# The L3 attention heads of a four-layer kernel: tiles handled in pairs, one reciprocal for two tiles

## The chip, the cores and the metric

The kernel runs on one core of a Trainium2 chip. The metric is the device time of one execution in microseconds (us): the median of 3 runs before the change is 2008.98 us (2007.1 to 2012.11).

## The reference, cut to what matters

Four conditioned layers, L0 to L3, follow each other on an activation of 2 x 1024 x 256. The change touches the attention of L3 alone:

```
qkv = (h @ Wqkv.T).reshape(b, n, 3, 16, 64)
q, k = _ln(q, qn_g, qn_b), _ln(k, kn_g, kn_b)        # per head, 64 wide
scores = einsum('bhnd,bhmd->bhnm', q, k) / sqrt(64)  # 1024 x 1024 per head
attn = softmax(scores, axis=-1)
o = einsum('bhnm,bhmd->bhnd', attn, v)               # then @ Wout.T, and a mixture of experts
```

There are 2 x 16 = 32 heads, each with a full 1024 x 1024 softmax over its rows.

## The kernel before

The stage `l3h` (class `Heads`, run by `heads_stage`) has one program for each engine. They run side by side and are tied only by semaphores. Its unit is a tile g: 128 query rows of one head against all 1024 keys. A head has TB = 8 tiles, and there are 256 tiles in all. For each tile:

- TensorE **scores** it (L1510): three passes of a high and low split of q and k, times two halves of the keys that stand on different rows of the array, into one of two score tiles in PSUM.
- VectorE takes the negated row maximum (L1567), ScalarE the exponential with the row sum (L1591), VectorE the reciprocal of the sum (L1573), and GpSimd scales the rows by it (L1601). The rows live in four slots of `prob`.
- TensorE **turns** it (L1521): 16 transposes of 64 rows x 128 columns, eight for each half of the rows. The halves go to two PSUM banks, `ring[0]` and `ring[1]`. VectorE copies one bank to `pT` (L1557), ScalarE the other (L1559).
- TensorE **mixes** (L1533): it multiplies a block of the turned rows with V, eight blocks kk for each head, into a result bank, which ScalarE copies out (L1581) and SyncE stores (L1479).

The order on each engine is written out by hand. Before, TensorE's loop over g does score(g), turn(g - 3), and the mix of the block 8 tiles behind the turn. VectorE does maximum g, reciprocal g - 1, copy g - 3. ScalarE does copy g - 3, exponential g. score(g) waits for the exponential of tile g - 2, whose score tile it overwrites. turn(g) waits until tile g is scaled and both banks of tile g - 1 are emptied.

SyncE's queue does, for each n: load q and k of head n + 1 (eight transfers, L1426 and L1427), store head n - 2, load V of head n + 1 (L1473). q and k have two buffers, and so has V. The load of V for head n + 1 first waits until `outs` counts n heads, that is until head n - 1 is mixed to its end. Only behind it in the same queue stand q and k of head n + 2. From n = 20 on, eight loads of finished heads for the next stage (L2069, `o3T`) stand in this queue too, one for each n. GpSimd has four pieces of weight splitting between its scalings, one each at tiles 40, 48, 56 and 64.

Of the kernel before, what the change touches and what calls it, by code (L numbers as in the profile page):

```python
# [18 lines left out]
ALU = mybir.AluOpType  # L19
ACT = mybir.ActivationFunctionType  # L20
AX = mybir.AxisListType

P = 128
B, S, D = 2, 1024, 256
T = B * S // P
TB = S // P
# [1085 lines left out]
def layer1_attention(nc, sems, g, w, nt):  # L1112
# [5 lines left out]
    with Stage(nc, sems, "l1att") as s:  # L1118
# [70 lines left out]
        @block.vector  # L1189
        def _(dve):  # L1190
            def empty(t):
                for half in range(2):
                    dve.wait_ge(his, 2 * t + half + 1)
                    dve.tensor_tensor(place(1, t, half), ring[half][:, :].rearrange("p (k q) -> p k q", k=TC),
                                      place(0, t, half).bitcast(F32), ALU.subtract).then_inc(emptied, 1)

            def residual(t):
                if t == 0:
                    dve.wait_ge(xbs, T)
                dve.reciprocal(inv[:, t:t + 1], total[:, t:t + 1]).then_inc(inverse, 1)  # L1200
                dve.wait_ge(outs, t + 1)
                dve.wait_ge(inverse, t + 1)
                dve.scalar_tensor_tensor(X[:, t, :], ob[t % 2][:, 0:D], inv[:, t:t + 1], X[:, t, :],
                                         ALU.mult, ALU.add).then_inc(added, 1)

            for t in range(T + 3):
                if t < T:
                    dve.wait_ge(scores, t + 1)
                    dve.tensor_reduce(nmax[:, t:t + 1], score[t % 2][:, :], AX.X, ALU.max, negate=True).then_inc(maxes, 1)
                if 1 <= t <= T:  # L1210
                    empty(t - 1)
                if t >= 3:
                    residual(t - 3)
                if T - 4 < t < T:
                    dve.wait_ge(added, (t - T + 4) * TC)
                    nt.dve_stats(dve, t - T + 3)
                if t == T:
                    nt.dve_norm(dve, 0)
# [210 lines left out]

class Heads:  # L1430

    LAG = 3
    N = B * H
    LOADS = 8

# [64 lines left out]
    def pe_program(self, pe):  # L1500
        def score(g):
            n, t = divmod(g, TB)
            u = n % 2
            if t == 0:
                self.need(pe, self.loaded[u], (n // 2 + u) * 16 * self.LOADS)
            self.need(pe, self.exps, g - 1)
            for i, (x, y) in enumerate(PASSES):
                for c in range(2):
                    r = slice(c * self.hd, (c + 1) * self.hd)
                    mm = pe.matmul(self.score[t % 2][:, c * C:(c + 1) * C], self.Q[u][r, x, t * P:(t + 1) * P],  # L1510
                                   self.K[u][r, y, :], start=i == 0, stop=i == 2)
            mm.then_inc(self.scores, 1)

        def turn(g):
            pe.wait_ge(self.scaled, g + 1)
            self.need(pe, self.emptied_d, g)
            self.need(pe, self.emptied_a, g)
            for kk in range(TB):
                for half in range(2):
                    r = slice(half * P // 2, (half + 1) * P // 2)  # L1520
                    mm = pe.transpose(self.ring[half][:, kk * P // 2:(kk + 1) * P // 2],  # L1521
                                      self.prob[r, g % 4, kk * P:(kk + 1) * P], self.ident[r, r])
                    if kk == TB - 1:
                        mm.then_inc(self.turned, 1)

        def mix(n, kk):
            if kk == 0:
                pe.wait_ge(self.emptied_d, TB * (n + 1))
                pe.wait_ge(self.emptied_a, TB * (n + 1))
                pe.wait_ge(self.vloaded[n % 2], 16 * (n // 2 + 1))  # L1530
                self.need(pe, self.ocopied, n - 1)
            for c in range(2):
                mm = pe.matmul(self.ob[n % 2][c * self.hd:(c + 1) * self.hd, :], self.vs[:, n % 2, kk, :],  # L1533
                               self.pT[:, n % 2, kk, c * C:(c + 1) * C], start=kk == 0, stop=kk == TB - 1)
            if kk == TB - 1:
                mm.then_inc(self.outs, 1)

        for g in range(TB * self.N + self.LAG + TB):
            if g < TB * self.N:
                score(g)  # L1540
            gt = g - self.LAG
            if 0 <= gt < TB * self.N:
                turn(gt)
            n, kk = divmod(gt - TB, TB)
            if n >= 0:
                mix(n, kk)

    def empty(self, eng, g, half):
        n, t = divmod(g, TB)
        eng.wait_ge(self.turned, 2 * g + half + 1)  # L1550
        if t == 0:
            self.need(eng, self.outs, n - 1)
        at = t * P + half * P // 2
        dst = self.pT[:, n % 2, :, at:at + P // 2]
        src = self.ring[half][:, :].rearrange("p (k q) -> p k q", k=TB)
        if half == 0:
            eng.tensor_copy(dst, src).then_inc(self.emptied_d, 1)  # L1557
        else:
            eng.activation(dst, src, ACT.Copy).then_inc(self.emptied_a, 1)  # L1559

    def dve_program(self, dve):
        for g in range(TB * self.N + self.LAG):
            if g < TB * self.N:
                t = g % TB
                dve.wait_ge(self.scores, g + 1)
                self.need(dve, self.exps, g - 3)
                dve.tensor_reduce(self.nmax[:, t % 4:t % 4 + 1], self.score[t % 2][:, :], AX.X, ALU.max,  # L1567
                                  negate=True).then_inc(self.maxes, 1)
            if 1 <= g <= TB * self.N:
                q = (g - 1) % 4  # L1570
                dve.wait_ge(self.exps, g)
                self.need(dve, self.scaled, g - 4)
                dve.reciprocal(self.inv[:, q:q + 1], self.total[:, q:q + 1]).then_inc(self.invs, 1)  # L1573
            if g >= self.LAG:
                self.empty(dve, g - self.LAG, 0)

    def act_program(self, act):
        def ocopy(n):
            act.wait_ge(self.outs, n + 1)
            self.need(act, self.stored[n % 2], 32 * (n // 2))  # L1580
            act.activation(self.osb[:, n % 2, :], self.ob[n % 2][:, :], ACT.Copy).then_inc(self.ocopied, 1)  # L1581

        for g in range(TB * self.N + self.LAG + 2 * TB):
            if self.LAG <= g < TB * self.N + self.LAG:
                self.empty(act, g - self.LAG, 1)
            if g < TB * self.N:
                q = g % 4
                act.wait_ge(self.maxes, g + 1)
                self.need(act, self.turned, 2 * (g - 3))
                self.need(act, self.invs, g - 3)  # L1590
                act.activation(self.prob[:, q, :], self.score[g % 2][:, :], ACT.Exp, bias=self.nmax[:, q:q + 1],  # L1591
                               accum_out=self.total[:, q:q + 1]).then_inc(self.exps, 1)
            n, k = divmod(g - 2 * TB, TB)
            if k == self.LAG - 1 and 0 <= n < self.N:
                ocopy(n)

    def pool_program(self, pool):
        for g in range(TB * self.N):
            q = g % 4
            pool.wait_ge(self.invs, g + 1)  # L1600
            pool.tensor_scalar(self.prob[:, q, :], self.prob[:, q, :], self.inv[:, q:q + 1], self.vscale,  # L1601
                               ALU.mult, ALU.mult).then_inc(self.scaled, 1)
            if g >= self.ROUND and g % TB == 0 and (g - self.ROUND) // TB < self.side.PIECES:
                self.side.pool_split(pool, (g - self.ROUND) // TB)
# [13 lines left out]
class NarrowPairs:  # L1618

    LAG = 2  # L1620
# [1630 lines left out]
```

## Time and profile before

| | |
|---|---|
| median of 3 runs | 2008.98 us |
| profiled execution, first to last instruction (its own time; what stands around it isn't in the profile) | 2000.0 us |
| PE busy | 1818.6 us (91%) |
| DVE busy | 1480.6 us (74%) |
| ACT busy | 1182.2 us (59%) |
| POOL busy | 813.1 us (41%) |
| the stage `l3h`, first score to last mix | 1107.7 to 1734.0 us |

The page gives the busy time of each engine over the whole span. PE is TensorE's matmuls, PEld its weight loads, DVE is VectorE, ACT ScalarE, POOL GpSimd, SP (SPq) SyncE. A line of a timeline gives start, duration, engine, source line, operation, the tile written <- the tiles read, and how often; in brackets the idle time before it and what ended that. Matmuls are pipelined, so the distance between two starts tells more of what one costs than the duration.

### The profile page before, as it was taken

To read this page: it belongs to the slowest core of one execution; us is meant where nothing else is said; L and a number is where in the kernel's file an instruction comes from. 1 tells how busy PE (TensorE), PEld (TensorE's weight loads), DVE (VectorE), ACT (ScalarE), POOL (GpSimd) and SP (SyncE) were. 2 spreads that over 40 slices of the span, in tenths; PEclk is the share of its full clock that TensorE was granted. 3 is DMA by queue.
4 is the path that set the end of the run, shared out by engine and by line. 5 is a ranking of instruction groups with operands and counts; after the bars stand their busy time and mean duration, and the time that the engine had idled before them with its cause. 6 is when DMAs were issued, how large, how long until landed. Compare 5 with 4: busy or idle time off the path is not lost. (4 is left out here: it accounts for less than half of the span.)

```text
span 2000.0 us, 37648 instructions
## 1 busy us (share of the span) xinstructions
PE 1818.6 (91%) x14478; PEld 1176.4 (59%) x14478; DVE 1480.6 (74%) x2537; ACT 1182.2 (59%) x2031; POOL 813.1 (41%) x736
## 2 busy tenths in 40 slices
PE   7998999899799989998998799999999999892886
PEld 5766699797333333346766455555555555582786
DVE  6676646647789899986887777777777777537796
ACT  3333233424177778875666777777777777523563
POOL 3464710554312120012666445544444444205576
PEclk9999999899589899999999899999999999995888
DMA  5000000202513112104669554454544555115452
GB/s 156 1 24 4 14 1 1 64 1 97 167 41 92 39 39 58 47 29 138 217 213 290 142 123 110 103 127 95 119 114 120 146 120 135 59 51 171 151 158 48
DMA packets 196195, 191.30 MB, mean 96 GB/s; under 512 B 64496, under 2 KB 154352, under 8 KB 195760
## 3 DMA queue, kind: packets, MB, share of 16 engines
q1 hardware_dynamic: 192944, 184.69, 34.1%
q0 software_dynamic: 3072, 4.20, 1.2%
q8 instruction: 115, 1.88, 0.4%
q14 instruction: 64, 0.52, 0.1%
HBM read 121.20 MB, written 67.37 MB: 94 GB/s over the span
## 5 line engine op out<-in xcount | busy, mean ns | idle before, releaser
L1601 POOL TENSOR_SCALAR l3h_prob<-l3h_prob,l3h_inv 128x1024 f32<-128x1024 f32 x256 | 287.1, 1121 | 322.5 <-DVE l3h_inv L1573 322.5
L1567 DVE TENSOR_REDUCE l3h_nmax<-l3h_score 128x1 f32<-128x1024 f32 x256 | 313.4, 1224 | 139.1 <-PE l3h_score L1510 139.0
L1801 DVE TENSOR_REDUCE l2h_nm<-l2h_rowb 128x1 f32<-128x1024 f32 x256 | 303.2, 1218 | 40.6 <-PE l2h_rowb L1733 40.1
L1851 ACT ACTIVATE l2h_pT<-l2h_score 128x512 f32<-128x512 f32 x512 | 273.8, 598 | 67.9 <-PE l2h_score L1749 49.7
L1591 ACT ACTIVATE l3h_prob<-l3h_score,l3h_nmax 128x1024 f32<-128x1024 f32 x256 | 285.8, 1116 | 37.7 <-DVE l3h_nmax L1567 2.7
L1533 PE MATMUL l3h_out<-l3h_pT,l3h_vs 128*64 128x512 f32 x1024 | 274.4, 617 | 0.0
L1559 ACT ACTIVATE l3h_pT<-l3h_ring 128x512 f32<-128x512 f32 x256 | 152.8, 597 | 106.4 <-PE l3h_ring L1521 105.9
L1521 PEld LDWEIGHTS l3h_ring<-ident,l3h_prob 64*128 64x128 f32 x4096 | 173.0, 138 | 35.5 <-issue 7.8
L1557 DVE COPY l3h_pT<-l3h_ring 128x512 f32<-128x512 f32 x256 | 172.0, 672 | 2.0 <-PE l3h_ring L1521 1.9
L1521 PE MATMUL l3h_ring<-ident,l3h_prob 64*128 64x64 f32 x4096 | 169.4, 222 | 2.2 <-DVE l3h_pT L1557 1.9
L1763 PE MATMUL l2h_out<-l2h_pT,l2h_vs 128*32 128x256 f32 (+1 forms) x1792 | 164.8, 443 | 0.0
L2650 POOL TENSOR_TENSOR l3qkv_lo<-l3qkv_full,l3qkv_hi 128x1024 fp32r<-128x1024 f32 x32 | 97.9, 3062 | 95.3 <-ACT l3qkv_hi L2547 95.3
L1510 PE MATMUL l3h_score<-k3first,q3first 64*128 64x512 f32 x768 | 124.2, 428 | 11.2 <-PEq L69 6.1
L1510 PEld LDWEIGHTS l3h_score<-k3first,q3first 64*128 64x128 f32 x768 | 63.1, 186 | 116.1 <-issue 96.3
L1510 PEld LDWEIGHTS l3h_score<-l3h_K,l3h_Q 64*128 64x128 f32 x768 | 62.1, 184 | 109.4 <-issue 95.1
L1510 PE MATMUL l3h_score<-l3h_K,l3h_Q 64*128 64x512 f32 x768 | 123.1, 425 | 2.8 <-DMA l3h_K<-l_k 2.6
L1733 PE MATMUL l2h_rowb<-l2K,l2Q 48*128 48x512 f32 x256 | 103.9, 502 | 12.1 <-PEq L69 8.3
L1749 PE MATMUL l2h_score<-l2Q,l2K 50*128 50x512 f32 x256 | 103.4, 492 | 2.5 <-DMA l2Q<-l2h_shift 1.1
L1865 POOL COPY l2h_vs<-V 128x128 f32<-128x128 f32 x32 | 8.3, 290 | 223.1 <-PE l2h_out L1763 223.1
L1295 POOL TENSOR_TENSOR l1mlp_y_lo<-l1mlp_y,l1mlp_y_hi 128x512 fp32r<-128x512 f32 x32 | 44.5, 1413 | 126.6 <-DVE l1mlp_y_hi L1407 126.6
L1733 PEld LDWEIGHTS l2h_rowb<-l2K,l2Q 48*128 48x128 f32 x256 | 45.5, 216 | 72.9 <-DVE l2h_nm L1801 57.0
L1763 PEld LDWEIGHTS l2h_out<-l2h_pT,l2h_vs 128*32 128x32 f32 x1792 | 36.3, 110 | 80.0 <-issue 50.5
(481 smaller groups left out, 4346.2 us busy)
## 6 DMA issues: line engine op xcount, KB each, us to landing
q3first<-l_q SPq DMA_DIRECT2D x64, 256.0 KB, 4.8
l3h_Q<-l_q SPq DMA_DIRECT2D x64, 256.0 KB, 4.9
l_q<-l3qkv_hi SPq DMA_DIRECT2D x16, 512.0 KB, 5.1
l_q<-l3qkv_lo SPq DMA_DIRECT2D x16, 512.0 KB, 4.5
l_k<-l3qkv_hi SPq DMA_DIRECT2D x16, 512.0 KB, 4.5
l_k<-l3qkv_lo SPq DMA_DIRECT2D x16, 512.0 KB, 3.3
k3first<-l_k SPq DMA_DIRECT2D x64, 128.0 KB, 5.0
l3h_vs<-l_v SPq DMA_DIRECT2D x32, 256.0 KB, 3.2
```

What stands on the lines that cost most here:

```text
L1510: mm = pe.matmul(self.score[t % 2][:, c * C:(c + 1) * C], self.Q[u][r, x, t * P:(t + 1) * P], self.K[u][r, y, :], start=i == 0, stop=i == 2)
L1521: mm = pe.transpose(self.ring[half][:, kk * P // 2:(kk + 1) * P // 2], self.prob[r, g % 4, kk * P:(kk + 1) * P], self.ident[r, r])
L1533: mm = pe.matmul(self.ob[n % 2][c * self.hd:(c + 1) * self.hd, :], self.vs[:, n % 2, kk, :], self.pT[:, n % 2, kk, c * C:(c + 1) * C], sta ...
L1557: eng.tensor_copy(dst, src).then_inc(self.emptied_d, 1)
L1559: eng.activation(dst, src, ACT.Copy).then_inc(self.emptied_a, 1)
L1567: dve.tensor_reduce(self.nmax[:, t % 4:t % 4 + 1], self.score[t % 2][:, :], AX.X, ALU.max, negate=True).then_inc(self.maxes, 1)
L1591: act.activation(self.prob[:, q, :], self.score[g % 2][:, :], ACT.Exp, bias=self.nmax[:, q:q + 1], accum_out=self.total[:, q:q + 1]).then_ ...
L1601: pool.tensor_scalar(self.prob[:, q, :], self.prob[:, q, :], self.inv[:, q:q + 1], self.vscale, ALU.mult, ALU.mult).then_inc(self.scaled, 1)
L1733: mm = pe.matmul(self.rowb[h][:, c * C:(c + 1) * C], self.Q[u][r:r + self.SPLIT, t * P:(t + 1) * P], self.K[u][r:r + self.SPLIT, c * C:(c ...
L1763: mm = pe.matmul(self.ob[r:r + self.mw, at:at + w], self.vs[:, m % self.SLOTS, h, k, :], self.pT[:, g % 4, h, c * C + at:c * C + at + w], ...
L1801: dve.tensor_reduce(self.nm[:, mr % 2, at:at + 1], self.rowb[h][:, :], AX.X, ALU.max, negate=True).then_inc(self.maxes, 1)
L1851: act.activation(self.pT[:, g % 4, h, c * C:(c + 1) * C], self.score[v % 3][:, :], ACT.Exp).then_inc(self.exps, 1)
```

## The change

All four compute engines now go over the tiles in pairs. LAG, the distance between score and turn, is 4 in place of 3. For an even g, TensorE does turn(g - 4), score(g), score(g + 1), turn(g - 3), and then two blocks of the mix. VectorE does copy g - 4, maximum g, one reciprocal over two columns (tiles g - 2 and g - 1), maximum g + 1, copy g - 3. ScalarE does copy g - 4, the result copy when one is due, copy g - 3, exponentials g and g + 1. GpSimd's scalings are as before, but wait for the pair's reciprocal. VectorE now copies row half 1 and ScalarE row half 0. `turn_bank` returns `ring[half]`, as the code read before. SyncE's program is unchanged.

```diff
-    LAG = 3
+    LAG = 4
@@ pe_program
         def turn(g):
+            if not 0 <= g < TB * self.N:
+                return
             pe.wait_ge(self.scaled, g + 1)
             self.need(pe, self.emptied_d, g)
             self.need(pe, self.emptied_a, g)
...
-        for g in range(TB * self.N + self.LAG + TB):
+        for g in range(0, TB * self.N + self.LAG + TB, 2):
+            turn(g - self.LAG)
             if g < TB * self.N:
                 score(g)
-            gt = g - self.LAG
-            if 0 <= gt < TB * self.N:
-                turn(gt)
-            n, kk = divmod(gt - TB, TB)
+                score(g + 1)
+            turn(g + 1 - self.LAG)
+            n, kk = divmod(g - self.LAG - TB, TB)
             if n >= 0:
                 mix(n, kk)
+                mix(n, kk + 1)
+
+    def turn_bank(self, g, half):
+        return self.ring[half]
@@ empty
-        if half == 0:
+        if half == 1:
             eng.tensor_copy(dst, src).then_inc(self.emptied_d, 1)
         else:
             eng.activation(dst, src, ACT.Copy).then_inc(self.emptied_a, 1)
@@ dve_program
+        def maximum(g):
+            dve.wait_ge(self.scores, g + 1)
+            self.need(dve, self.exps, g - 3)
+            dve.tensor_reduce(self.nmax[:, g % 4:g % 4 + 1], self.score[g % 2][:, :], AX.X, ALU.max,
+                              negate=True).then_inc(self.maxes, 1)
+
+        def inverses(g):
+            q = g % 4
+            dve.wait_ge(self.exps, g + 2)
+            self.need(dve, self.scaled, g - 2)
+            dve.reciprocal(self.inv[:, q:q + 2], self.total[:, q:q + 2]).then_inc(self.invs, 1)
+
+        for g in range(0, TB * self.N + self.LAG, 2):
+            self.empty(dve, g - self.LAG, 1)
             if g < TB * self.N:
...
+                maximum(g)
+            if 2 <= g <= TB * self.N:
+                inverses(g - 2)
+            if g < TB * self.N:
+                maximum(g + 1)
+            self.empty(dve, g + 1 - self.LAG, 1)
@@ act_program
+        def exponents(g):
+            q = g % 4
+            act.wait_ge(self.maxes, g + 1)
+            self.need(act, self.turned, 2 * (g - 3))
+            self.need(act, self.invs, g // 2 - 1)
+            act.activation(self.prob[:, q, :], self.score[g % 2][:, :], ACT.Exp, bias=self.nmax[:, q:q + 1],
+                           accum_out=self.total[:, q:q + 1]).then_inc(self.exps, 1)
+
+        for g in range(0, TB * self.N + self.LAG + TB + 2, 2):
+            self.empty(act, g - self.LAG, 0)
+            n, k = divmod(g - self.LAG - 2 * TB, TB)
+            if n >= 0 and k == 0:
+                ocopy(n)
+            self.empty(act, g + 1 - self.LAG, 0)
             if g < TB * self.N:
...
+                exponents(g)
+                exponents(g + 1)
@@ pool_program
-            pool.wait_ge(self.invs, g + 1)
+            pool.wait_ge(self.invs, g // 2 + 1)
```

## Rows read from the trace of the kernel before

**Rows 1.** The page: busy times, and one costly group (busy us, mean ns).
```profile
PE 1818.6 (91%) x14478; PEld 1176.4 (59%) x14478; DVE 1480.6 (74%) x2537; ACT 1182.2 (59%) x2031; POOL 813.1 (41%) x736
...
L1510 PE MATMUL l3h_score<-l3h_K,l3h_Q 64*128 64x512 f32 x768 | 123.1, 425 | 2.8 <-DMA l3h_K<-l_k 2.6
```

**Rows 2.** Busy time by window (stretch, its us, PE, PEld, DVE, ACT, POOL, PEclk, DMA, GB/s).
```profile
1200.00:1400.00 200.00, 200.00 (x2168) 113.65 (x2166) 157.26 (x252) 155.52 (x262) 101.04 (x92) 1.00 0.47 109
```

**Rows 3.** Timeline of one tile in the steady stretch: start, us, engine, line, operation.
```profile
1303.33 0.67 DVE L1557 COPY l3h_pT<-l3h_ring 128x512 f32<-128x512 f32 x1
1303.38 1.12 ACT L1591 ACTIVATE l3h_prob<-l3h_score,l3h_nmax 128x1024 f32<-128x1024 f32 x1
1303.51 1.12 POOL L1601 TENSOR_SCALAR l3h_prob<-l3h_prob,l3h_inv 128x1024 f32<-128x1024 f32 x1 [1.27 <-DVE l3h_inv L1573]
...
1303.52 0.96 PE L1510 MATMUL l3h_score<-k3first,q3first 64*128 64x512 f32 x6
...
1304.32 0.66 PE L1521 MATMUL l3h_ring<-ident,l3h_prob 64*128 64x64 f32 x16
...
1304.52 1.22 DVE L1567 TENSOR_REDUCE l3h_nmax<-l3h_score 128x1 f32<-128x1024 f32 x1 [0.52 <-PE l3h_score L1510]
...
1304.90 1.08 PE L1533 MATMUL l3h_out<-l3h_pT,l3h_vs 128*64 128x512 f32 x4
...
1305.66 0.15 DVE L1573 RECIPROCAL l3h_inv<-l3h_total 128x1 f32<-128x1 f32 x1
1305.73 0.67 DVE L1557 COPY l3h_pT<-l3h_ring 128x512 f32<-128x512 f32 x1
...
1305.91 0.96 PE L1510 MATMUL l3h_score<-k3first,q3first 64*128 64x512 f32 x6
```

**Rows 4.** Timeline of the stage's first tiles, which have no mix yet.
```profile
1117.64 0.67 DVE L1557 COPY l3h_pT<-l3h_ring 128x512 f32<-128x512 f32 x1
...
1118.41 0.72 PE L1521 MATMUL l3h_ring<-ident,l3h_prob 64*128 64x64 f32 x16 [0.43 <-DVE l3h_pT L1557]
...
1118.95 0.96 PE L1510 MATMUL l3h_score<-k3first,q3first 64*128 64x512 f32 x6
...
1119.43 0.67 DVE L1557 COPY l3h_pT<-l3h_ring 128x512 f32<-128x512 f32 x1
...
1120.02 1.21 DVE L1567 TENSOR_REDUCE l3h_nmax<-l3h_score 128x1 f32<-128x1024 f32 x1
...
1121.15 0.15 DVE L1573 RECIPROCAL l3h_inv<-l3h_total 128x1 f32<-128x1 f32 x1
```

**Rows 5.** Timeline of the stage's end: the last turn, then nine mixes in a row.
```profile
1725.42 0.71 PE L1521 MATMUL l3h_ring<-ident,l3h_prob 64*128 64x64 f32 x16
...
1726.07 7.95 PE L1533 MATMUL l3h_out<-l3h_pT,l3h_vs 128*64 128x512 f32 x36
```

**Rows 6.** SyncE's own waits, 1130 to 1700: total us, times, longest.
```profile
SPq L1473 <- PE l3h_out L1533: 357.4, 29, 20.8
```

**Rows 7.** Timeline of one head's loads (V; last part of K) and first score.
```profile
1492.89 0.36 SPq L1473 DMA_DIRECT2D l3h_vs<-l_v  x1
...
1497.77 0.60 SPq L1427 DMA_DIRECT2D l3h_K<-l_k  x1
...
1504.78 0.95 PE L1510 MATMUL l3h_score<-l3h_K,l3h_Q 64*128 64x512 f32 x6
```

**Rows 8.** DMA issues: the last K part issued at 1171.96, then at 1497.77; us to landing.
```profile
k3first<-l_k SPq DMA_DIRECT2D x1, 128.0 KB, 5.0
...
l3h_K<-l_k SPq DMA_DIRECT2D x1, 128.0 KB, 6.6
```

**Rows 9.** Timeline: V loads that open and close the eight heads with o3T loads.
```profile
1512.07 0.37 SPq L1473 DMA_DIRECT2D l3h_vs<-l_v  x1
...
1524.98 0.96 PE L1510 MATMUL l3h_score<-k3first,q3first 64*128 64x512 f32 x6 [0.98 <-DMA k3first<-l_k]
...
1671.34 0.36 SPq L1473 DMA_DIRECT2D l3h_vs<-l_v  x1
```

More of the change, by code:

```diff
@@ L1520, in turn @@
                     r = slice(half * P // 2, (half + 1) * P // 2)
-                    mm = pe.transpose(self.ring[half][:, kk * P // 2:(kk + 1) * P // 2],
+                    mm = pe.transpose(self.turn_bank(g, half)[:, kk * P // 2:(kk + 1) * P // 2],
                                       self.prob[r, g % 4, kk * P:(kk + 1) * P], self.ident[r, r])
@@ L1536, in mix @@
                 mm.then_inc(self.outs, 1)
-        for g in range(TB * self.N + self.LAG + TB):
+        for g in range(0, TB * self.N + self.LAG + TB, 2):
+            turn(g - self.LAG)
             if g < TB * self.N:
                 score(g)
-            gt = g - self.LAG
-            if 0 <= gt < TB * self.N:
-                turn(gt)
-            n, kk = divmod(gt - TB, TB)
+                score(g + 1)
+            turn(g + 1 - self.LAG)
+            n, kk = divmod(g - self.LAG - TB, TB)
             if n >= 0:
                 mix(n, kk)
+                mix(n, kk + 1)
+    def turn_bank(self, g, half):
+        return self.ring[half]
     def empty(self, eng, g, half):
+        if not 0 <= g < TB * self.N:
+            return
         n, t = divmod(g, TB)
@@ L1554, in empty @@
         dst = self.pT[:, n % 2, :, at:at + P // 2]
-        src = self.ring[half][:, :].rearrange("p (k q) -> p k q", k=TB)
-        if half == 0:
+        src = self.turn_bank(g, half)[:, :].rearrange("p (k q) -> p k q", k=TB)
+        if half == 1:
             eng.tensor_copy(dst, src).then_inc(self.emptied_d, 1)
@@ L1561, in dve_program @@
     def dve_program(self, dve):
-        for g in range(TB * self.N + self.LAG):
-            if g < TB * self.N:
[L1564 to L1575, printed above, removed]
+        def maximum(g):
[10 more added lines that the diff above has]
+            self.empty(dve, g - self.LAG, 1)
+            if g < TB * self.N:
+                maximum(g)
[4 more added lines that the diff above has]
+            self.empty(dve, g + 1 - self.LAG, 1)
     def act_program(self, act):
@@ L1581, in ocopy @@
             act.activation(self.osb[:, n % 2, :], self.ob[n % 2][:, :], ACT.Copy).then_inc(self.ocopied, 1)
-        for g in range(TB * self.N + self.LAG + 2 * TB):
-            if self.LAG <= g < TB * self.N + self.LAG:
-                self.empty(act, g - self.LAG, 1)
-            if g < TB * self.N:
[L1587 to L1595, printed above, removed]
+        def exponents(g):
[11 more added lines that the diff above has]
+            self.empty(act, g + 1 - self.LAG, 0)
+            if g < TB * self.N:
+                exponents(g)
+                exponents(g + 1)
     def pool_program(self, pool):
```

## The prediction

> **What bounds the kernel now.** I read the page first, then the busy time by window, the timeline of a steady tile, the timelines of the stage's two ends, where kinds of work stand next to each other that don't in the middle, and last the waits of SyncE's own queue with the landing times of its loads.
>
> TensorE is the busiest engine [rows 1] and has no idle time at all in the stage's steady stretch [rows 2]. A tile takes 1305.91 - 1303.52 = 2.39 us [rows 3]: score to turn 0.80, turn to mix 0.58, mix to the next score 1.01. VectorE's loop ends close by: the copy of 1303.33 ends at 1304.00, and the transposes that need its bank start at 1304.32; the maximum starts 0.04 after the score's end (1303.52 + 0.96) and only then does the next reciprocal and copy follow. So TensorE's order of work sets 2.39, with VectorE 0.2 to 0.3 behind the limit.
>
> The second clock of the stage is less visible. SyncE waits 357.4 us in 29 places at the V load for the mix [rows 6]; the q and k loads of the head after next stand behind it. For the head of [rows 7], V is issued at 1492.89, when a head has just been mixed, the eighth part of q and k at 1497.77, and it lands 6.6 later [rows 8], at 1504.37. Its first score stands at 1504.78, just in time. I call X the time from the V issue to the last landing and its receipt (0.05, an estimate from the stalled head below). For this head X = 4.88 + 6.6 + 0.05 = 11.5, the time until the score 11.89. Five tiles (5 x 2.39 = 11.95) lie between. The 18 heads before the o3T loads have landings of 5.0 to 6.6 (the first and the last of them in [rows 8]), X from 9.9 to 11.5, mean 10.9, so none stalls. The eight heads with an o3T load in the queue do: the first has X = 1524.98 - 1512.07 = 12.91 and stalls; V to V over the eight is (1671.34 - 1512.07) / 8 = 19.91 [rows 9] against 8 x 2.393 = 19.15, a mean stall of 0.76, hence a mean X of 12.6.
>
> **The change part by part.** *TensorE's work.* With t = 0 at the first transpose of turn(g - 4) the pair runs: that turn, 0.53 to the next score (1118.41 to 1118.95 [rows 4]); score g 0.80 [rows 3]; score g + 1, whose weights load behind a running score. One score matmul lasts 0.43 [rows 1] of the group's 0.96, so the first two of three passes take some 0.55 and the third, with its load hidden, some 0.25. For the second score I take 0.70, between 0.65 and the 0.80 of an unhidden start. Then turn(g - 3) 0.58 and two mixes. Nine mixes in a row take 7.95 [rows 5]: less the last matmul's 0.6, 17 steps of 0.43, 0.86 for a mix, where one alone costs 1.01. The pair of mixes costs 0.86 + 1.01 = 1.87. Sum 0.53 + 0.80 + 0.70 + 0.58 + 1.87 = 4.48, against 4.79 for two tiles before: 0.31 less.
>
> The page "TensorE: Matmul & The Clock Gate" of the Trainium skill (section "Step-by-step: what each phase is for") says that the reorder window pulls the next weight load ahead of running matmuls. By that alone grouping alike work would save nothing and the pair would stay at 4.79. The trace differs at a change of kind: 1.01 for a mix before a score, 0.86 before a mix.
>
> *VectorE's loop.* turn(g - 2) opens the next pair and needs copy g - 3, which now is the last thing VectorE does in a pair. From t = 0: score g starts at 0.53, ends at 1.49, maximum g starts at 1.53. A reciprocal follows a maximum's start by 1.13 (1120.02 to 1121.15) and the next instruction it by 0.07 (1305.66 to 1305.73) [rows 3, 4]: maximum g + 1 at 2.73, copy g - 3 at 3.86, ended 4.53, the first transpose 0.10 later (copy ended 1118.31, transpose 1118.41 [rows 4]) at 4.63. So p = 4.63 a pair: the loop, not TensorE's 4.48, becomes the bound, and 4.79 - 4.63 = 0.16 is left of the gain. The bounds are 4.48 and 4.79.
>
> *The rest of the waits.* The second exponential ends about 5.54 (copy g - 3 at 2.75, then 0.5, 1.10 and 1.20 for the two exponentials with their sums), and score g + 3 at 4.63 + 1.33 = 5.96 needs it: 0.4 to spare. GpSimd scales from 2.9 to 5.2 and turns need it at 4.6 and 6.7. One reciprocal in place of two is hidden in GpSimd's idle 1.27 [rows 3] and saves VectorE 0.07 a pair, counted above. The swap of row halves and `turn_bank` cost nothing: the two banks and the two copies are the same, beside TensorE's work. Four weight pieces on GpSimd now delay the second scaling of their pairs: 0 to 3, I take 0.5.
>
> *SyncE's loads.* Nothing is changed there, but both ends of their window move. A head's last block is now mixed in the pair 8h - 6. V is issued when the pair's last matmul ends: 0.53 + 0.80 + 0.70 + 0.58, then 0.48 + 2 x 0.43 to its start, 0.6 and 0.05, t = 4.60. The first score of head h comes after turn(8h - 4) in pair 8h: 3p + 0.53 = 14.42. The window shrinks from 11.89 to 9.82. Every head but the shortest has X above that, so each stalls for X - 9.82 after the turn, with VectorE's loop standing behind the same score: nothing absorbs it. A head takes 4p + X - (3p + 0.53 - 4.60) = X + p + 4.07. Note that p weighs only once.
>
> For the 18 heads and the last two (without o3T): 10.9 + 4.63 + 4.07 = 19.60, +0.45 each on 19.15, 20 of them +9.0. For the eight: 12.6 + 8.70 = 21.3, +1.4 each on 19.91, +11.2.
>
> *The ends.* Before the first mix a tile takes 1.79 (copy to copy [rows 4]), since TensorE has little to do; VectorE's loop now makes it 2.32: six tiles, +3.2 (0 to 6). In the drain, turns come in pairs with a copy between them (0.7 to end, 0.67 copied, 0.10) and no mix to cover it: +1.5 (0 to 3).
>
> Sum: 9.0 + 11.2 + 3.2 + 1.5 + 0.5 = +25.4. The profiled span of 2000.0 becomes 2025; the median of the runs lies 9 above that span, so 2009 becomes 2034.
>
> **The rivals.** *Loads stay hidden.* If X falls below 9.82, or V is issued sooner, only p decides: 122 pairs with mixes x 0.16 = -19, the ends +5, the o3T stalls as before: 1995. It decides at X = 9.82. For it: at the fastest head X is 9.9. Against: 17 of 18 are above, and what makes X (eight issues in one queue, the landing) isn't touched. If VectorE's loop didn't bind either it would be -38 + 5, 1976. The skill's "Perfetto Trace Analysis" ("Identifying Performance Opportunities") speaks for this side: improve the most-contended engine. That engine is TensorE here, and its work does shrink.
>
> *TensorE's pair saves nothing* (0.86 holds in the drain alone, or ScalarE's 0.4 to spare is used up by the result copy): p = 4.79, V at 4.75, a head costs X + 4.79 + 4.22, 0.31 x 28 = +9 on the forecast: 2043.
>
> *No net change.* X about 0.7 shorter than before, since the loads then fall on other work, gives 28 x 0.7 = -20: 2014 or less with a smaller start: within 0.3% of before, about 2011. I see no row for it.
>
> **How the numbers follow.** Forecast (heads stall for q and k) 0.80, its own range 2020 to 2046, from X +-0.3 on 28 heads (+-8), p and the pair's terms (-4, +5) and the ends (-5, +5). TensorE saves nothing 0.06; loads hidden 0.08; no net change 0.06. A measurement of this kernel can tell 0.3%, 6 us, from no change. Faster 0.08, same 0.06, slower 0.86. The range reaches down to 2014 for part of the last rival and up to 2048 for the second.
>
> **What would show it.** Right: score starts of a pair 0.80 apart and then 3.8; pairs of 4.6 inside a head, one stall at every eighth tile, put down to the k or q load, of 0.5 to 1.7 and of 2 to 3.5 in the eight heads; V to V about 19.6 and 21.3; mixes of a pair 0.91 and 0.96 apart; the first transpose of a pair 0.1 behind the end of a copy. Wrong: pairs at 4.48 (VectorE's loop is shorter), pairs over 4.8 (a wait I didn't see, first the exponential's), or heads without a load wait, which would turn the sign.

## The result, and the profile after

The changed kernel takes 2042.25 us (median of 4 runs, 2039.23 to 2046.08) against 2008.04 us (the median of before with a fourth run); the ratio is 1.0178 with the interval 1.0137 to 1.022. It is slower, as forecast (2034, ratio 1.0125). The profiled execution spans 2039.8 us. Its stage of the heads, first score to the end of the last mix, grew from 626.3 to 659.5 us. The other 6.6 us of the spans' difference stand where nothing was changed, 3.0 less ahead of the stage and 9.6 more behind it: that work took 266 to 278 us over the ten profiles of this case, and the profile of before has the shortest.

The page after, busy times, against [rows 1]:

```profile
PE 1802.5 (88%) x14478; PEld 1203.1 (59%) x14478; DVE 1472.0 (72%) x2409; ACT 1144.7 (56%) x2031; POOL 812.5 (40%) x736
```

TensorE is busy for 16 us less and the kernel is longer. By window (stretch, its us, PE, PEld, DVE, ACT, POOL, PEclk, DMA, GB/s), against [rows 2]:

```profile
1200.00:1400.00 200.00, 186.03 (x2122) 115.16 (x2119) 150.27 (x204) 137.14 (x254) 96.04 (x89) 1.00 0.45 107
...
1470.00:1720.00 250.00, 223.61 (x2426) 137.78 (x2422) 173.97 (x235) 158.73 (x292) 103.32 (x94) 0.95 0.47 115
```

In the same 200 us TensorE stood 14 us idle where it had stood none, and in the second half of the stage (the second row) its granted clock wasn't full. The timeline of one head boundary, against [rows 3, 7]:

```profile
1302.33 0.68 DVE L1565 COPY l3h_pT<-l3h_ring 128x512 f32<-128x512 f32 x1
...
1303.11 0.71 PE L1523 MATMUL l3h_ring<-ident,l3h_prob 64*128 64x64 f32 x16
...
1303.60 1.66 PE L1510 MATMUL l3h_score<-k3first,q3first 64*128 64x512 f32 x12
...
1305.08 0.68 PE L1523 MATMUL l3h_ring<-ident,l3h_prob 64*128 64x64 f32 x16
...
1305.69 1.94 PE L1535 MATMUL l3h_out<-l3h_pT,l3h_vs 128*64 128x512 f32 x8
...
1307.67 0.36 SPq L1473 DMA_DIRECT2D l3h_vs<-l_v  x1
...
1307.72 0.71 PE L1523 MATMUL l3h_ring<-ident,l3h_prob 64*128 64x64 f32 x16
...
1313.68 0.60 SPq L1427 DMA_DIRECT2D l3h_K<-l_k  x1
...
1316.96 0.71 PE L1523 MATMUL l3h_ring<-ident,l3h_prob 64*128 64x64 f32 x16
...
1318.16 1.23 PEld L1510 LDWEIGHTS l3h_score<-l3h_K,l3h_Q 64*128 64x128 f32 x12 [0.63 <-DMA l3h_K<-l_k]
1318.16 1.66 PE L1510 MATMUL l3h_score<-l3h_K,l3h_Q 64*128 64x512 f32 x12 [0.49 <-DMA l3h_K<-l_k]
```

A pair lasts 1307.72 - 1303.11 = 4.61 us. VectorE's copy ends at 1303.01 and the first transpose follows after 0.10. V is issued at 1307.67, the last part of K at 1313.68; that part lands 4.4 later (below) at 1318.1, and the score starts right behind it. After turn(g - 4) the score could have started at 1316.96 + 0.49 = 1317.45: 0.7 us are lost. Two more rows: SyncE's wait at the V load (1130 to 1740), and the landing of that last part (DMA issues: KB, us to landing), against [rows 8]:

```profile
SPq L1473 <- PE l3h_out L1535: 397.4, 30, 26.2
```

```profile
l3h_K<-l_k SPq DMA_DIRECT2D x1, 128.0 KB, 4.4
```

SyncE's wait tells nothing of the loss: over 1130 to 1700, the stretch of [rows 6], it is 357.5 us here and 357.4 there. What tells it is TensorE's wait. The waits of the score line after (us, times):

```profile
  DMA l3h_K<-l_k: 40.7, 28
  DMA k3first<-l_k: 35.0, 28
```

Weight loads and matmuls are counted apart there, 56 times for 28 heads: all but head 7 of the 29 from head 3 on. Before, there were 23 such entries. 15 of them are from the eight heads with an o3T load; the other eight are weight loads that stood idle for 0.81 us, as they did before every first score, and cost nothing.

### The profile page after: what moved, and what is told of

It is laid out like the page before. It is cut to its first block and busy times, and to the rows that moved or that the text cites. A ratio compares the mean times of both kernels' runs of the same rounds, so it can differ in the third digit from the quotient of the medians.

```text
span 2039.8 us, 37394 instructions
## 1 busy us (share of the span) xinstructions
PE 1802.5 (88%) x14478; PEld 1203.1 (59%) x14478; DVE 1472.0 (72%) x2409; ACT 1144.7 (56%) x2031; POOL 812.5 (40%) x736
## 3 DMA queue, kind: packets, MB, share of 16 engines
q1 hardware_dynamic: 192944, 184.69, 33.2%
q8 instruction: 115, 1.88, 0.4%
## 5 line engine op out<-in xcount | busy, mean ns | idle before, releaser
L1523 PEld LDWEIGHTS l3h_ring<-ident,l3h_prob 64*128 64x128 f32 x4096 | 168.2, 141 | 142.6 <-POOL l3h_prob L1620 121.6
L1535 PE MATMUL l3h_out<-l3h_pT,l3h_vs 128*64 128x512 f32 x1024 | 251.1, 613 | 0.0
L1523 PE MATMUL l3h_ring<-ident,l3h_prob 64*128 64x64 f32 x4096 | 180.6, 227 | 22.0 <-DVE l3h_pT L1565 8.3
L1510 PE MATMUL l3h_score<-k3first,q3first 64*128 64x512 f32 x768 | 110.7, 418 | 24.2 <-DMA k3first<-l_k 16.5
L1510 PE MATMUL l3h_score<-l3h_K,l3h_Q 64*128 64x512 f32 x768 | 110.1, 416 | 19.5 <-DMA l3h_K<-l_k 19.4
L1535 PEld LDWEIGHTS l3h_out<-l3h_pT,l3h_vs 128*64 128x64 f32 x1024 | 63.6, 138 | 86.9 <-issue 78.2
L1510 PEld LDWEIGHTS l3h_score<-k3first,q3first 64*128 64x128 f32 x768 | 75.5, 192 | 34.6 <-DMA k3first<-l_k 18.5
L1510 PEld LDWEIGHTS l3h_score<-l3h_K,l3h_Q 64*128 64x128 f32 x768 | 75.3, 191 | 29.0 <-DMA l3h_K<-l_k 21.3
```

The source lines that it names most:

```text
L1523: mm = pe.transpose(self.turn_bank(g, half)[:, kk * P // 2:(kk + 1) * P // 2], self.prob[r, g % 4, kk * P:(kk + 1) * P], self.ident[r, r])
```

## The experiments

**V behind q and k.** In all runs named "v_behind" SyncE issues each V load one turn of its queue later. q and k then wait only until the buffer's last reader has scored.

```diff
-            if n + 1 < self.N:
-                load_v(n + 1)
+            if 1 <= n < self.N:
+                load_v(n)
```

In the changed kernel (pairs_v_behind):

> The paired kernel, with one edit in SyncE's program: the V load of a head is issued one turn of the queue later, so that q and k of the next head but one no longer stand behind a V load that waits for the mix. Theory (the pair costs its time because heads stall for q and k): no head waits for a load, V's own wait is never the last one, pairs of 4.61 us throughout, 28 heads x 18.45 in place of 568 us, the stage 50 us shorter than in the paired kernel, and faster than the kernel before by about 20: 1985 to 1992 us. Rival (the pairs themselves are slow, or the loads are late for their own length of 10 to 13 us): 2035 to 2045, with waits for q and k still in the rows. If the lower clock stretches of the paired kernel's stage follow from its stalls, they vanish too; if they belong to the pairs, six to eight of them stay.

Measured: 1984.42 us (12 runs), ratio to before 0.9893 (0.9859 to 0.9928). The stage takes 608.4 us, 51 less than in the changed kernel. Its timeline, with the first turns of two pairs, the copy that frees the second, a V load and the next q load:

```profile
1301.99 0.71 PE L1523 MATMUL l3h_ring<-ident,l3h_prob 64*128 64x64 f32 x16
...
1304.97 0.59 SPq L1473 DMA_DIRECT2D l3h_vs<-l_v  x1
...
1305.83 0.68 DVE L1565 COPY l3h_pT<-l3h_ring 128x512 f32<-128x512 f32 x1
...
1306.61 0.71 PE L1523 MATMUL l3h_ring<-ident,l3h_prob 64*128 64x64 f32 x16
...
1308.80 0.46 SPq L1426 DMA_DIRECT2D q3first<-l_q  x1
```

SyncE's waits in it, 1130 to 1700 (us, times, longest):

```profile
SPq L1479 <- ACT l3h_osb L1596: 260.7, 30, 16.7
SPq L1426 <- PE l3h_score L1510: 98.5, 29, 13.3
```

The pair is 4.62 as before, V's wait for the mix is gone, no score waits for a load, and V to V is 18.48, four pairs. TensorE's clock is at 1.00 from 1150 to 1470 and at 0.99 from there to 1740, 26 us past the stage's end: from head 3 on, the changed kernel's six stretches at the lower clock are gone with the stalls. The theory holds; the rival (the pairs are slow) falls.

In the kernel before (before_v_behind):

> The kernel before, with the same edit of the V load alone. Theory: its heads hardly wait for q and k, only the eight with an o3T load do, 6 us in all, so it becomes 5 to 6 us faster than before: ratio 0.997, about 2003. Rival (the queue's order was worth as much in the kernel before, so that the run with pairs says nothing about pairs): 20 us or more faster.

Measured: 1997.59 us (12 runs), 0.9944 (0.9911 to 0.9978), the stage 620.3, 6.0 less, and V to V is 19.16 at every head. The ratio lets it be 0.2 to 0.9%, the stage says 6 us as forecast. So the kernel before had next to nothing of this wait, and the pairs themselves, freed of it, are worth 620.3 - 608.4 = 11.9 us.

**LAG alone.** Single tiles as before, and LAG 4 in place of 3:

> The kernel before, single tiles as they were, with LAG = 4 in place of 3 alone. The last mix of a head and so the issue of V, q and k come one tile (2.39 us) later against the head's first score, so the window shrinks from 11.9 to 9.5. Theory: 20 heads stall for 1.4 on the mean, the eight with an o3T load for 2.4 more than before, two short: +45 us, 2045 to 2060, and the waits are put down to q and k. Rival (pairing, not the window, made the time; ring banks, orders on VectorE): within 5 us of before.

Measured: 2067.35 us (4 runs), 1.0272 (1.0215 to 1.033), the stage 685.2. One head boundary in its timeline:

```profile
1314.52 0.36 SPq L1473 DMA_DIRECT2D l3h_vs<-l_v  x1
...
1319.71 0.60 SPq L1427 DMA_DIRECT2D l3h_K<-l_k  x1
...
1325.23 0.97 PE L1510 MATMUL l3h_score<-l3h_K,l3h_Q 64*128 64x512 f32 x6 [1.18 <-DMA l3h_K<-l_k]
```

V to score is 10.71 and the wait 1.2, where the row of before had none at 11.89 [rows 7]. The 18 heads without an o3T load average 20.2 V to V for 19.15; I had put 20.5. The time lies above the range that I had given (2045 to 2060): among the eight heads with o3T loads the clock fell too (0.93 from 1540 to 1740), and seven of them are longer, between the last landing and the next V, than the heads without a fall, by 1.4 to 2.8 us each, 12 in all. The later mix alone, with nothing paired, costs more than the whole change.

The same with V behind:

> The kernel before with LAG = 4 and the V load one turn of the queue later. Theory: the window of q and k no longer hangs on the mix, so LAG costs nothing: as the kernel before with the later V load, 2000 to 2006. Rival (LAG = 4 costs in another way, through the four row slots or the exponential's wait for the turn): over 2015.

Measured: 1999.88 us (10 runs), 0.9961 (0.9928 to 0.9993), the stage 621.5, 1.2 more than with LAG 3. LAG costs through the load queue and, beyond that 1.2, nowhere else.

**What sets the pair.** The runs from here on are all on the changed kernel with V behind, the first three of them one execution each. First, more work on VectorE:

```diff
                 maximum(g + 1)
+            for i in range(3):
+                dve.reciprocal(self.spare[:, 2 * g + i:2 * g + i + 1], self.ident[:, 0:1])
             self.empty(dve, g + 1 - self.LAG, 1)
```

> The paired kernel with V behind, and three more small reciprocals on VectorE (of a constant, into a tile that nothing reads) between the second maximum and the second copy of each pair. Each is followed by the next instruction after 0.07. Theory (VectorE's chain from the first score to the second copy sets the pair, 4.61): the pair becomes 4.61 + 3 x 0.07 = 4.82 us, the stage 608 + 26 = 634. Rival TensorE (its own 4.48 plus something unseen sets 4.61): 4.61 stays, or 4.7 at most. Rival GpSimd (the profile's rows put the first turn's wait down to its scaling): 4.61 stays, since its scalings come before the added work.

```profile
1401.25 0.71 PE L1524 MATMUL l3h_ring<-ident,l3h_prob 64*128 64x64 f32 x16 [0.28 <-issue]
...
1406.05 0.71 PE L1524 MATMUL l3h_ring<-ident,l3h_prob 64*128 64x64 f32 x16 [0.28 <-issue]
```

These are the first turns of two pairs in its timeline, 4.80 apart for 4.62, and the stage is 631.4 (23 more). The three reciprocals take 0.19 from the first's start to the copy's. Then less work on TensorE (the third pass of every odd tile's score is left out):

> The paired kernel with V behind, and the second tile of each pair scored in two passes in place of three (the last pass of the high and low split is left out for every odd tile). TensorE has 0.23 less to do in a pair. Theory (VectorE's chain): the second score isn't in it, since the second maximum waits for the first, so the pair stays at 4.61 and the stage at 608. Rival TensorE: 4.38, the stage 29 us shorter.

```profile
1400.43 0.72 PE L1524 MATMUL l3h_ring<-ident,l3h_prob 64*128 64x64 f32 x16 [0.33 <-issue]
...
1405.05 0.71 PE L1524 MATMUL l3h_ring<-ident,l3h_prob 64*128 64x64 f32 x16 [0.34 <-issue]
```

Here they are 4.62 apart and the stage is 611.6, with nothing gained. Work on VectorE ahead of the second copy is paid in full, and a shorter second score, which isn't in VectorE's chain, buys nothing: that chain, from the first score to the second copy, is the bound. GpSimd is named in the rows of the first turn's wait, as in this one of the changed kernel:

```profile
1303.08 0.60 PEld L1523 LDWEIGHTS l3h_ring<-ident,l3h_prob 64*128 64x128 f32 x16 [0.94 <-POOL l3h_prob L1620]
```

It isn't the cause: its two scalings run from 1301.38 to 1303.59, the first of them, which this turn needs, ends at 1302.5, and the copy at 1303.01. The wait has three semaphores, and the copy is the last to come.

**The row halves as before:**

> The paired kernel with V behind, the two row halves given to VectorE and ScalarE as in the kernel before (VectorE half 0, ScalarE half 1). Both theories: nothing, the pair at 4.61 and the stage at 608 within 2 us; at most 0.01 a pair, since half 1 is ready 0.007 later. More than 5 us would mean that the swap was a part of the time.

Measured: first turns 4.62 apart, the stage 608.0. The swap costs nothing.

**A version that should gain more.** VectorE copies tile g - 3 ahead of the second maximum:

> The paired kernel with V behind, and VectorE copies the second turned tile ahead of the second maximum. The copy leaves the chain to the next pair's turn; in its place the second maximum is late by 0.6, and its exponential must end before the second score of the next pair: second score 0.70, turned 0.66 and 0.04, copy 0.59, maximum 1.22, exponential with its sum 1.24, 0.03 to the score = 4.48. TensorE's own work is 4.48 too. Theory: the pair goes from 4.61 to 4.48 to 4.52, the stage from 608 to 592 to 597, the kernel to 1969 to 1974. Rival (ScalarE, whose copy, result copy and exponentials now stand closer together, takes over): 4.6 or above, no gain.

Measured: 1996.44 us (12 runs), 0.9935 (0.9903 to 0.9968), the stage 609.0: no gain on 608.4, where I had expected 592 to 597. Its timeline:

```profile
1404.91 0.72 PE L1523 MATMUL l3h_ring<-ident,l3h_prob 64*128 64x64 f32 x16
...
1405.04 1.12 ACT L1603 ACTIVATE l3h_prob<-l3h_score,l3h_nmax 128x1024 f32<-128x1024 f32 x1 [0.20 <-DVE l3h_nmax L1573]
...
1405.44 1.82 PE L1510 MATMUL l3h_score<-k3first,q3first 64*128 64x512 f32 x12
...
1406.30 0.53 PEld L1510 LDWEIGHTS l3h_score<-k3first,q3first 64*128 64x128 f32 x6 [0.35 <-ACT l3h_prob L1603]
...
1407.10 0.65 PE L1523 MATMUL l3h_ring<-ident,l3h_prob 64*128 64x64 f32 x16
...
1407.68 1.94 PE L1535 MATMUL l3h_out<-l3h_pT,l3h_vs 128*64 128x512 f32 x8
...
1409.55 0.65 PE L1523 MATMUL l3h_ring<-ident,l3h_prob 64*128 64x64 f32 x14
```

The pair is 4.64. The second score's weight load waits 0.35 for the exponential. The matmuls run on without a gap, but the two scores take 1.66 (1405.44 to 1407.10) in place of 1.48: the load isn't hidden behind the first score any more. TensorE is full (249.60 of 250 us busy from 1150 to 1400), with 0.17 more to do. The chain through the second tile has no slack either: weight load to turn 0.80, to the copy 0.72, to the maximum 0.61, to the exponential 1.25, to the next second score's weight load 1.26, 4.64 in all. My sum of 4.48 for that chain had 0.70 at its first step. The rival gave the right number (4.6 or above) for a wrong reason: the second exponential waits 0.20 for its maximum, and not for ScalarE's other work. The faster version of this case is pairs_v_behind.

## Why the prediction was right, point by point

- *TensorE's work for a pair, 4.48.* The distances are 0.49 from turn to score (I had 0.53), 1.48 for two scores (1.50), 0.61 from turn to mix (0.58). The eight matmuls of two mixes last 1.94, 1.35 without the last one's 0.59, and a mix's last start stands 0.53 before the next work (1.01 - 0.48 in [rows 3]): 1.88 (1.87). Sum 4.46.
- *VectorE's chain sets p = 4.63.* It is 4.61 to 4.62, and both runs on the bound (more on VectorE, less on TensorE) say the same.
- *The window of q and k shrinks to 9.82.* V to the earliest score is 1307.67 to 1317.45, 9.78. Every head waits: in all 29 from head 3 on, the first score starts 0.04 behind the last landing. (In head 7 TensorE is hardly idle, since a weight piece on GpSimd had delayed the turns of that window.) The mean X from the landings of the 28 heads 4 to 31 is 11.3 after, 11.4 before; so the loads were hardly touched, as assumed.
- *Heads 4 to 31.* From the first score of head 3 to that of head 31 it is 568.5 us in place of 542.6, +25.9, where the sum had +20.2. With X + p + 4.07 and the measured X and p it is 559.4, so stalls and pairs alone come to +16.8, 3.4 less than forecast: X was 10.8 on the mean in the 18 heads and 12.4 in the eight with an o3T load, where I had 10.9 and 12.6. The remaining 9.1 are the term that I didn't have: TensorE's clock. Head by head, 22 of the 28 are X + p + 4.07 to within 0.01. The six others are 1.2 to 2.5 longer, 9.2 together, and they are the six whose window from V to V has a clock under 1.00. Two neighbours with X = 12.4 each:

```profile
1657.03:1678.12 21.09, 18.31 (x208) 11.44 (x208) 14.82 (x20) 13.61 (x26) 8.84 (x9) 1.00 0.50 126
1678.12:1700.58 22.46, 19.77 (x208) 12.00 (x208) 14.82 (x20) 13.68 (x26) 8.84 (x9) 0.92 0.47 118
```

The window below, right behind the stall of an o3T head (one of the eight with an o3T load in the queue), is at 1.2 of the two levels, 1.2 and 2.4 GHz:

```profile
1559.40:1565.00 5.60, 5.57 (x34) 3.52 (x36) 3.10 (x4) 1.75 (x4) 2.21 (x2) 0.50 0.02 4
```

and the two scores behind it last 2.93, elsewhere 1.67 (timeline of the same kernel):

```profile
1559.43 2.93 PE L1510 MATMUL l3h_score<-l3h_K,l3h_Q 64*128 64x512 f32 x12 [2.65 <-DMA l3h_K<-l_k]
...
1571.16 1.67 PE L1510 MATMUL l3h_score<-l3h_K,l3h_Q 64*128 64x512 f32 x12
```

- *The ends.* The start costs +5.9 to the first score of head 3 (I took 3.2 of 0 to 6), the drain +1.4 (1.5). In the start are head 3's stall of 1.3, which I hadn't counted, and two stretches at the lower clock. pairs_v_behind has such two as well, no stall, and +4.4.
- *GpSimd's weight pieces.* Four heads of pairs_v_behind take 18.84 for 18.48: 1.5 for my 0.5. In the changed kernel the same four heads fit X + p + 4.07, so there the pieces cost nothing: the wait for q and k covers them.
- *The rivals.* "Loads stay hidden" gave 1995 as the time without the wait; pairs_v_behind, which is that case made true for the o3T heads too, has 1984. "TensorE's pair saves nothing" (2043) would have met the time by chance: its p = 4.79 isn't in the rows.

In sum, the sign and the mechanism were right, and the size of the stalls nearly so (+16.8 for +20.2 with the pairs' gain in it). The stage grew by 33.2 where I had 25.4. The 7.8 between them are: clock behind the stalls +9.1, start +2.7, stalls -3.4, pieces -0.5, drain -0.1. That the time is only 8 us above the forecast is partly luck, since the last three errors offset a third of the first two. The clock is a term that the sum put at nothing without a reason.

One step was wrong without effect, since the +25.4 is a difference and can be added to the median itself: that the median lies 9 us above a profiled span. The changed kernel's profiled execution took 2041.54 us for its 2039.8 of span, 1.7 more. The profile of before was only a fast execution of a kernel whose runs lie 15 us apart.

## What to carry to other kernels

Regrouping work on the compute engines moves the events that an unchanged DMA queue waits for. For each load, take the distance from the event that lets it go to its first reader, in the new order, and compare it with the landing time in the trace. In this kernel's queue the q and k loads, whose own buffers were free, stood behind V's wait for the mix, and issuing V one turn of the queue later took 51 us off the stage. And look at who is second: once the pairs took about 0.3 of 4.79 us from TensorE's work, VectorE's chain kept half of it.

## What was not expected of the hardware

Waits of 1.4 to 2.7 us, at most one in a head, with TensorE busy for 223.61 of 250 us around them, came with stretches at 1.2 GHz. From head 3 to head 31 such stretches occur in the changed kernel and in before_lag4 (waits of 2.6 to 4.1 in its eight o3T heads), the two in which every head stalls, and in none of the other profiles. The kernel before kept its full clock through stalls of up to 1.2 us. The changed kernel's clock is full from 1150 to 1470, with 15 waits of 0.2 to 1.6 us:

```profile
1150.00:1470.00 320.00, 300.08 (x3410) 185.87 (x3408) 242.61 (x328) 223.97 (x413) 153.13 (x140) 1.00 0.47 109
```

Which wait brings it down isn't settled. After 1.42 us at 1475.63 the clock fell, after 2.47 at 1648.34 and 2.40 at 1669.44 it didn't.
